# A transformer kernel on one Trainium2 core: its first stage in another order, and 343 TensorE wait instructions put elsewhere

## The reference

```
res = x
h = _layer_norm(x, ln1_scale, ln1_offset)
x = res + _cross_attention(h, xf_1, ...)      # attention layer 0
res = x
h = _layer_norm(x, ln2_scale, ln2_offset)
x = res + _cross_attention(h, xf_2, ...)      # attention layer 1
...
qh = (q_in @ wq + bq).reshape(b, q_len, H, K)   # H = 16 heads of K = 128
kh = (kv_in @ wk + bk)...                       # + one more key, bias_k
vh = (kv_in @ wv + bv)...                       # + one more value, bias_v
weights = softmax(qh kh / sqrt(K))
x = (weights vh) @ wo + bo
```

## Time and profile before

| | us |
|---|---|
| median of 3 runs | 1558.56 (1557.78 to 1559.69) |
| profiled execution, its own time | 1559.04 |
| its span, first to last instruction | 1557.3 |
| TensorE busy | 1505.2 |
| VectorE busy | 973.1 |
| ScalarE busy | 866.4 |
| GpSimd busy | 413.4 |

### The profile page before, as it was taken

One profiled execution on the slowest core, in us unless ns is written; L12 is line 12 of the kernel. 1 busy time (PEld: TensorE's weight loads), 2 busy tenths in 40 slices (PEclk: granted clock), 3 DMA queues, 4 the chain that ended last, 5 costly groups with the idle time before them and its releaser, 6 DMA issues. The chain is left out here.

```text
span 1557.3 us, 41338 instructions
## 1 busy us (share of the span) xinstructions
PE 1505.2 (97%) x17264; PEld 1305.5 (84%) x17264; DVE 973.1 (62%) x2135; ACT 866.4 (56%) x1626; POOL 413.4 (27%) x445
## 2 busy tenths in 40 slices
PE   8899999999999999999999999999999999999996
PEld 7688888888888788888888888988878888888864
DVE  7746546554566664555646676479996558865366
ACT  5454353354455554454453466577777567775476
POOL 1320120210201510210210123036774206542052
PEclk9999999999999999999999999999999999999998
DMA  6010010010010010010010000020002000000001
GB/s 214 1 69 2 29 42 1 29 43 1 29 42 1 29 42 2 29 42 2 29 43 29 29 2 28 1 83 2 3 29 82 1 29 3 30 2 28 8 22 55
DMA packets 17832, 46.20 MB, mean 30 GB/s; under 512 B 1360, under 2 KB 11616, under 8 KB 14704
## 3 DMA queue, kind: packets, MB, share of 16 engines
q1 hardware_dynamic: 13456, 39.33, 7.3%
q10 hardware_dynamic: 4192, 4.24, 0.8%
HBM read 39.37 MB, written 4.19 MB: 28 GB/s over the span
## 5 line engine op out<-in xcount | busy, mean ns | idle before, releaser
L174 PE MATMUL ps<-ch,W 128*128 128x512 f32 (+1 forms) x2484 | 582.9, 384 | 12.7 <-DVE arena L1346 6.0
L174 PEld LDWEIGHTS ps<-ch,W 128*128 128x128 f32 x2484 | 437.8, 189 | 98.3 <-issue 5.9
L174 PEld LDWEIGHTS ps<-W,split_arena 128*128 128x128 f32 x3084 | 388.4, 188 | 23.5 <-issue 4.7
L174 PE MATMUL ps<-W,split_arena 128*128 128x256 f32 x3084 | 401.9, 283 | 3.4 <-DVE split_arena L1678 2.6
L1343 DVE TENSOR_REDUCE small<-ps 128x4 f32<-128x260 f32 x128 | 53.9, 421 | 241.3 <-PE ps L774 241.1
L1184 ACT ACTIVATE arena<-ps,hbias 128x512 f32<-128x512 f32 x128 | 87.9, 688 | 206.6 <-PE ps L174 205.6
L174 PE MATMUL ps<-W,ch 128*128 128x512 f32 (+1 forms) x864 | 193.7, 381 | 0.3
L1169 ACT ACTIVATE arena<-ps 64x256 f32<-64x256 f32 x256 | 96.8, 378 | 170.2 <-PE ps L860 166.4
L174 PEld LDWEIGHTS ps<-W,ch 128*128 128x128 f32 x864 | 154.6, 188 | 31.8 <-ACT arena L2166 0.9
L1678 DVE TENSOR_TENSOR split_arena<-arena,split_arena 128x512 fp32r<-128x512 f32 x96 | 72.1, 751 | 124.8 <-ACT split_arena L1710 115.0
L1370 DVE TENSOR_TENSOR x_sb<-ps,x_sb 128x512 f32<-128x512 f32 x128 | 87.0, 689 | 97.4 <-PE ps L174 97.2
(11 more groups left out here) (172 smaller groups left out, 2020.4 us busy)
## 6 DMA issues: line engine op xcount, KB each, us to landing
raw<-wpack SPq DMA_DIRECT2D x23, 1028.0 KB, 4.8
rows<-vb_in SPq DMA_DIRECT2D x8, 512.0 KB, 5.7
x_sb<-x_in SPq DMA_DIRECT2D x4, 512.0 KB, 9.7
arena<-ctxT SPq DMA_DIRECT2D x4, 512.0 KB, 9.9
spill<-x_sb ACTq DMA_DIRECT2D x1, 2048.0 KB, 11.3
arena<-spill ACTq DMA_DIRECT2D x1, 2048.0 KB, 8.3
arena<-ctx_tok SPq DMA_DIRECT2D x16, 128.0 KB, 2.0
out<-x_sb SPq DMA_DIRECT2D x7, 256.0 KB, 2.5
```

The lines of the kernel that those rows point to most:

```text
L174: last = e.matmul(dst, lhs[a], rhs[b], start=start and n == 0, stop=stop and n == 2, skip_group_check=True)
```

## The change

- TensorE, waits: each instruction of a regular block now needs one wait at most. Waits that another wait implies are left out (the keys' in `pe_scores`, the values' and probabilities' in `pe_heads`), others ride on a matmul that has none. A regular block is then 592 instructions, or 688 with values, and four in a row are 2560.
- TensorE, filling: `idle(e, n)` issues n instructions that only wait for none_ok, which is long set. There are 163 at the start, ahead of the warm-up, and 30 behind each of six value tiles in `pe_block_after`. They make up exactly for the 343 that went: both programs have 35,235 TensorE instructions.
- Opening: of the context's low parts, chunks 2 and 3 go from VectorE to GpSimd. The normalizing of chunks 1 to 3 goes from VectorE to ScalarE (`act_tiles`); VectorE makes the negative mean for it (`dve_mean`). The orders of TensorE, ScalarE and VectorE are changed to suit, and a query's first matmuls wait for half of a norm's low part only.
- Turn: VectorE takes value tiles in another order among the norm's steps, GpSimd makes two powers (`pool_pow`) ahead of the row additions, and `pe_block_after` has its last norm between value tiles.
- `pe_singles`: ScalarE copies the queries ahead of the second step's probabilities.

```diff
-        def context_dve(e, c):
+        def context_lo(e, c):
...
-                e.wait_ge(second_mean, c + 1)
+                e.wait_ge(second_mean, l * NCH + c)
...
         def pe_scores(e, t):
-            if t % NCH == 0:
-                e.wait_ge(a_kb, t // NCH + 1)
             for h in range(2):
-                e.wait_ge(a_ke, two(t, h))
                 e.wait_ge(a_qe, two(t, h))
                 for n in range(BPC):
+                    if (t + 1) % NCH == 0 and t + 1 < STEPS and h == 1 and n == 4:
+                        pack_ready(e, t + 1, 0)
...
+        def pe_query(e, u, h, also=None, seen=0):
+            for k in range(KT):
+                if u % LAYER < NCH and h == 0:
+                    e.wait_ge(norm0.s["lo"].sem, norm0.s["lo"].at((u // LAYER * NCH + u % NCH) * KT + k))
+                if k and also is not None:
+                    e.wait_ge(also, seen)
+                ins = pe_project(e, u, k, 0, hT, query_bank(u) + h, h)
...
         def pe_heads(e, t):
-            e.wait_ge(a_ve, values_done(t, TPC - 1))
-            e.wait_ge(a_pt, two(t, 1))
...
+        PAGE_START, PAGE_TURN = 163, 30
+        def idle(e, n):
+            for _ in range(2 * n):
+                e.wait_ge(none_ok, 1)
...
         def pe_block_after(e):
             for i in range(2):
                 e.wait_ge(a_ke, two(b, i))
                 pe_values(e, a, i)
+                idle(e, PAGE_TURN)
             e.wait_ge(a_acc, two(a - 4, 1))
             for i in range(2):
                 pe_values(e, a, 2 + i)
+                idle(e, PAGE_TURN)
...
-            for i in range(TPC):
+            for i in range(2):
                 e.wait_ge(a_ve, values_done(a, i))
                 pe_values(e, b, i)
+                idle(e, PAGE_TURN)
+            e.wait_ge(a_ve, values_done(a, TPC - 1))
+            pe_norm(e, 1, 3)
             e.wait_ge(a_ol, two(a - 2, 1))
-            pe_norm(e, 1, 3)
+            for i in range(2):
+                pe_values(e, b, 2 + i)
...
         def pe_attend(e):
+            idle(e, PAGE_START)
             e.wait_ge(none_ok, 1)
             for n in range(WARM):
...
             act_keys(e, 0)
             act_norm(e, 0, 0)
             context_act(e, 1)
+            first_act(e, 4)
             act_queries(e, 0)
-            first_act(e, 4)
+            context_act(e, 2)
+            norm0.act_tiles(e, 1, 0)
...
             act_probs(e, SINGLE - 2)
+            act_queries(e, SINGLE)
             act_probs(e, SINGLE - 1)
-            act_queries(e, SINGLE)
...
             dve_add(e, b - 4)
+            dve_values(e, a, (1,))
             dve_stats(e, 1, 1)
-            dve_values(e, a, (1,))
+            dve_values(e, b, (0,))
             dve_mean(e, 1, 1)
+            dve_values(e, b, (1,))
             norm0.dve_lo(e, 0, 1)
...
             norm0.pool_pow(e, 1)
+            e.wait_ge(c_lo.sem, c_lo.at(KT + KT - 1))
+            context_lo(e, 2)
             norm0.pool_pow(e, 2)
+            context_lo(e, 3)
             norm0.pool_pow(e, 3)
```

More of the change, by code:

```diff
@@ L832, in pe_values @@
         def pe_values(e, t, i):
-            if t % NCH == 0 and i == 0:
-                wait(e, v_half, t // NCH // 2)
             a = (t % NCH * TPC + i) * P
             for nth, k in enumerate((1, 0)):
+                if t % NCH == 0 and i == 0 and k == 0:
+                    wait(e, v_half, t // NCH // 2)
                 if t == 0 and i == 0:
@@ L842, in pe_values, with pe_out @@
             ins.then_inc(a_V, 1)
-        def pe_out(e, t):
+        def pe_out(e, t, keys=None):
             w, b = W[t // NCH % 2], out_bank(t)
@@ L847, in pe_out @@
                 pack_ready(e, t, 4)
-            e.wait_ge(a_ol, two(t, 1))
             for j in range(2):
+                if j and keys is not None:
+                    e.wait_ge(a_ke, two(keys, 1))
                 for i in range(2):
@@ L900, in pe_visit @@
             pe_heads(e, a - 2)
-            wait(e, a_acc, two(b - 4, 1))
             pe_heads(e, b - 2)
@@ L908, in pe_upper @@
             a, b = 2 * d, 2 * d + 1
-            behind = values_behind(d - 1)
-            if behind:
+            if values_behind(d - 1):
                 pe_values_behind(e, d - 1)
-            for h in range(2):
-                if behind:
+                for h in range(2):
                     e.wait_ge(a_ve, values_done(a - 2, h))
[L915 to L918, removed]
+                    pe_key(e, a, h)
+                for h in range(2):
                     e.wait_ge(a_ve, values_done(b - 2, h))
-                e.wait_ge(a_ol, two(a - 4, 1))
[L921 to L928, removed]
+                    pe_key(e, b, h)
+                pe_out(e, a - 4)
+                e.wait_ge(a_ve, values_done(b - 2, TPC - 1))
+                pe_out(e, b - 4, a)
+            else:
+                for h in range(2):
+                    e.wait_ge(a_sub, two(a - 2, h))
+                    pe_key(e, a, h)
+                e.wait_ge(a_ol, two(a - 4, 1))
+                for h in range(2):
+                    pe_key(e, b, h)
+                e.wait_ge(a_sub, two(b - 2, 1))
+                pe_out(e, a - 4)
+                e.wait_ge(a_ol, two(b - 4, 1))
+                pe_out(e, b - 4, a)
             for i in range(2):
-                e.wait_ge(a_ke, two(a, i))
                 pe_transpose(e, a - 2 + i)
@@ L939, in pe_queries @@
             for h in range(2):
-                e.wait_ge(a_acc, two(a - 4, h))
-                pe_query(e, b, h)
+                e.wait_ge(a_acc, two(a - 4, 1) if h == 0 else two(b - 4, 1))
+                if h == 0 and a % NCH == 0:
+                    pe_query(e, b, h, a_kb, a // NCH + 1)
+                elif h == 1:
+                    pe_query(e, b, h, a_pt, two(b - 2, 1))
+                else:
+                    pe_query(e, b, h)
         def pe_block(e, d):
@@ L975, in pe_block_first @@
                 pe_query(e, 1, h)
+            e.wait_ge(a_ke, two(1, 1))
+            pe_norm(e, 0, 2)
+            e.wait_ge(a_kb, 1)
             e.wait_ge(a_ve, values_done(1, TPC - 1))
@@ L1028, in pe_block_turn @@
             e.wait_ge(a_qe, two(a, 1))
+            e.wait_ge(a_pt, two(b - 2, 1))
             pe_heads(e, a - 2)
@@ L1093, in pe_singles @@
             e.wait_ge(a_sub, two(t - 1, 1))
+            e.wait_ge(a_ol, two(t - 3, 1))
             pe_out(e, t - 3)
+            e.wait_ge(a_ol, two(t - 2, 1))
             pe_out(e, t - 2)
@@ L1100, in pe_singles @@
             e.wait_ge(a_acc, two(t - 2, 1))
+            e.wait_ge(a_pt, two(t - 1, 1))
             pe_heads(e, t - 1)
+            e.wait_ge(a_ke, two(t, 1))
             pe_scores(e, t)
@@ L1145, in pe_attend @@
             next0.lead(e)
+            e.wait_ge(a_ol, two(STEPS - 2, 1))
             pe_out(e, STEPS - 2)
@@ L1149, in pe_last_values, with act_norm @@
         def pe_last_values(e):
+            e.wait_ge(a_pt, two(STEPS - 1, 1))
             pe_heads(e, STEPS - 1)
         def pe_last_out(e):
+            e.wait_ge(a_ol, two(STEPS - 1, 1))
             pe_out(e, STEPS - 1)
         WARM = 16
-        def act_norm(e, l, c, parts=range(2 * KT)):
+        def act_norm(e, l, c, parts=(0, 2, 1, 3)):
             b = norm_banks(l, c)
@@ L1585, in pool_attend @@
                     split_half(e, n)
-            for c in range(NCH):
-                norm0.pool(e, c, row("bo2"), 1)
+            for c in (0, 2):
+                norm0.pool_pow(e, c, 1)
+                norm0.pool_pow(e, c + 1, 1)
+                norm0.pool_row(e, c, row("bo2"), 1)
+                norm0.pool_row(e, c + 1, row("bo2"), 1)
             for n in range(NHP + 1, 2 * NHP + 1):
```

86 lines of the change are left out of this document (43 added, 43 removed).

## The result

The changed kernel takes 1567.95 us (median of 5 runs, 1566.88 to 1568.94), the kernel before beside it 1559.69. The ratio is 1.0053, interval 1.0039 to 1.0068: slower by 8.3 us. The forecast was 1571, in the range 1555 to 1582.

The account below looks back on a forecast made before the run. TensorE, busy 1505.2 of 1557.3 us, was taken as the bound. From 1558.6 us: opening +10.4, block after the turn +7.6 and +0.5, pages -4.1, turn -2.1, end -0.2, sum +12.1; forecast 1571, range 1555 to 1582.

Parts of the forecast that it names:

- Pads: TensorE's filling waits: pitch 0.11 us each, so the 163 at the start delay the first keys by 17.6 us.
- Rivals 1 (cheap): Satisfied waits follow at their 51 ns, at the start and value tiles: 1552 us, 1543 if free; chance 17%.
- 2 (dearer): Pads at 0.15 us, as at the release: start 6.5 us more, value tiles 7, total 1584 us; chance 8%.
- step a: Block after the turn, four padded value tiles: the first loses 0.7 us, the others 2.0 each, 6.6 in all.
- step b: Block after the turn, two padded value tiles behind short matmuls with nothing queued: a loss of 3.9 us.
- Opening: Start of the kernel: +17.6 us for pads, -10.9 for stalls removed, +3.7 for new lateness, +10.4 in all.
- one of my signs: Opening: a sign of the forecast being right was no idle time over 1 us before the first maximum.
- the context part that I had costed at nothing: Opening: GpSimd's context parts are needed some 10 us after they can be made, so they cost nothing.
- Pages: Instruction-page stalls around the scores' bursts: 9.2 us before, 5.1 after, so 4.1 saved, ends 0 and 9.
- The place 37 and 293: Page boundaries counted from a burst's start: a stall of 0.65 us each, between 0 and 1.3, seven times.
- Rival 4: Page stalls stay, because fetches wait for the DMA queues or boundaries do not matter: 1575 us; chance 9%.
- Turn: First turn block: sixth value copy 0.5 us sooner, clock may stay up; -2.1 us together, ends 0 and -4.

Follow-up runs that it names:

- spread: Changed kernel with the same 163 and 180 pads placed behind single matmuls (warm-up and long ones): 1544.8 us, ratio to the kernel before 0.9909.
- pool_later: On spread, GpSimd's turn bias rows wait for VectorE's means of both chunks, its opening context part for the mean of chunk 1: 1539.21 us.
- eight_fewer: On spread, 8 of the 115 pads behind the opening's long matmuls left out, nothing else: 1551.85 us, 7.05 slower than spread.
- after: The changed kernel itself, as profiled, with 163 pads ahead of the warm-up and 30 behind each of six value tiles: 1567.95 us.
- two_each: As spread, same number of pads, but two behind each long matmul on half as many matmuls: 1550.35 us.
- three_each: As spread, but three pads behind each of about 91 long matmuls: 1557.23 us.
- pads_419: Changed kernel with 419 pads instead of 163 ahead of the warm-up, one page more: 1595.93 us.
- no_start: Changed kernel without the 163 pads ahead of the warm-up: 1558.15 us.
- no_turn: Changed kernel without the 180 pads in the block after the turn: 1564.45 us.
- no_pads: Changed kernel with neither group of pads, only the new order and the thinned waits: 1557.0 us.

## Why the prediction was right, and where it was not

- **Pads.** Taken at 0.11 us, with 0.051 and 0.15 as ends. Measured 0.106 from start to start in most of the pairs, 0.108 over all 163. Rivals 1 (cheap) and 2 (dearer) are settled by the first keys at 25.23.
- **Where they cost.** Right in both places: 17.0 us at the start (predicted 17.6), and behind the value tiles. From start to start the gaps grew by 0.66, 1.80, 1.80 and 1.90 in step a (predicted 6.6 in all, measured 6.2) and by 1.68 and 1.98 in step b (3.9, measured 3.7). Of these 9.8 us 7.2 remained, so 2.7 were recovered against them, predicted 2.9. Against spread, the same order with its pads hidden, step a's pads cost 6.4 us and step b's only 0.1, since TensorE would have waited there anyway. spread shows the other side too: the same pads are free behind long matmuls.
- **Opening.** -10.9 + 3.7 predicted, -7.6 measured to the first heads. The stalls that remained were 1.3, 1.4 and 1.0 us (by gap), at the second norm's transposes, at the second query and at the transposes of the probabilities. I had 0, 0.2 and 1.6 there, and 0.8 at the first heads, where none came. So that the sum fits is in part luck, and one of my signs failed: two idle times over 1 us stand ahead of the first maximum. The first stall was the context part that I had costed at nothing. GpSimd was not late with it; it held up VectorE, and pool_later takes it away.
- **Pages.** This is the term that was mis-sized: "The place 37 and 293 lies beside these; I take 0.65". It costs nothing, as do 133 and 389. The price is no slope that can be read between 38 (0) and 45 (1.3); it is a step between 40 and 44. Where the fetch of the first boundary starts decides, and the prediction did not ask for that. The term was -4.1 and came out at -8.5, at its good end. Rival 4, that boundaries do not matter, is refuted by eight_fewer: eight instructions fewer, nothing else, and 6 us of stalls.
- **Turn.** That the sixth value copy "comes only 0.5 sooner" failed: it came 0.8 later, because two powers in a row let GpSimd's rows fall beside VectorE's small steps. That the clock may stay was right for this run only. With the same wait of 3.0 us it stayed at 1.00 in after, spread, two_each, three_each and pads_419, and fell to 0.50 for 3.4 us in no_start, no_turn, no_pads and eight_fewer, at some 1.45 us each. What decides between these is open. The same wait in after and in no_turn (us, busy of PE, PEld, DVE, ACT, POOL, clock, DMA share, GB/s):

```profile
483.00:487.00 4.00, 4.00 (x22) 3.42 (x22) 1.23 (x2) 3.28 (x6) 1.54 (x3) 1.00 0.00 0
...
483.00:487.00 4.00, 4.00 (x16) 3.27 (x15) 1.46 (x3) 3.28 (x5) 1.32 (x2) 0.62 0.00 0
```

The errors of pages (-4.4) and turn (+1.5) partly cancel; with the smaller ones +12.1 was 4.1 us too high. The forecast was only 3 us high, because the kernel before took 1.1 us more beside the changed one (1559.69) than in the runs that it was worked out from (1558.56).

## What to carry to other kernels

In this kernel filling that only moves code cost its pitch where the sequencer had no queued work ahead of the engine, and nothing, with small exceptions, behind an operation that lasts longer than it. Where short matmuls run faster than pages of instructions arrive, count where the boundaries fall, move them with hidden filling, and measure a single place before pricing it by its neighbours. Work given to an idle GpSimd has two prices that its own lateness does not show: what it holds up on VectorE beside it, and what stands behind it in its own queue.

## What the runs showed of the hardware

- An instruction of TensorE's queue that waits for a set semaphore has a duration of 51 ns in the profile and a pitch of 106 ns in most pairs, and of 108 to 109 ns over rows of 163 and 256 (after, pads_419).
- The price of a second boundary in a burst of 384 instructions jumps from at most 0.2 us to 0.7 to 2.0 us between places 40 and 44 of the first, with the start of the fetch; the stall ends 1.2 to 1.7 us behind the recorded end of that fetch, which itself takes 0.9 to 1.6 us. Why the crossing moves by more than a microsecond within four instructions is open. The Trainium skill ("Runtime: NRT & Kernel Launch", "Instruction fetch mechanics") calls the crossing mostly hidden; that holds here for 512-column work, and in bursts by place only.
- VectorE's small steps of 0.16 us in the reciprocal root (L508 to L514, all operands in SBUF) took 0.62 to 0.67 us beside GpSimd's rows (0.7 each) and 1.12 to 1.22 beside its context parts (1.27 each), that is, about one GpSimd instruction. The value copies, which read PSUM, kept 0.41 beside the same rows (476.95 in the trace before). The Trainium skill ("SBUF — State Buffer", "SBUF: two separate sides") describes one port pair shared by the two engines, held exclusively for a whole instruction; the durations of the steps that were held up agree. It names VectorE operations with two SBUF inputs or in a 2-port mode; the step with a single tensor input (L512, 0.67) was held up as well, and whether it ran in such a mode no trace shows. A step of the same kind and size (L486) kept its 0.17 us beside the rows of the trace before:

```profile
467.66 2.82 POOL L409 TENSOR_TENSOR x_sb<-x_sb,rows 128x256 f32<-128x256 f32 x4 [3.66 <-ACT norm_arena L554]
...
469.68 0.17 DVE L486 TENSOR_SCALAR small<-small 128x4 f32<-128x4 f32 x1
```
